# Soft experts of a vision tower: one mixing block per image instead of two, and the down products spread as three per image instead of six per second image

## The reference

```python
slots = jnp.einsum('bnd,bnes->besd', x, dispatch)
h = jax.nn.gelu(jnp.einsum('besd,edh->besh', slots, w1) + b1[None, :, None, :])
y = jnp.einsum('besh,ehd->besd', h, w2) + b2[None, :, None, :]
out = jnp.einsum('besd,bnes->bnd', y, combine)
```

## Time and profile before

| | us |
|---|---|
| median of 3 runs | 1109.38 |
| the runs | 1108.49, 1109.38, 1493.33 |
| the profiled execution | 1109.79 |
| its span (first to last instruction) | 1108.0 |
| soft experts: first hidden matmul to the start of the last down products | 241.06 to 665.51 |
| TensorE busy (share of the span) | 987.2 (89%) |
| ScalarE busy | 661.1 (60%) |
| VectorE busy | 390.4 (35%) |

### The profile page before, as it was taken

The page is one execution under the profiler, slowest core; times in us unless marked ns, Lnnn a source line. Parts: engine busy times, 40 slices in busy tenths (PEclk is TensorE's granted clock), DMA queues, the critical chain, the costliest instruction groups (busy, mean ns, idle before and its releaser), DMA issues. The chain is left out here.

```text
span 1108.0 us, 20060 instructions
## 1 busy us (share of the span) xinstructions
PE 987.2 (89%) x7464; PEld 646.1 (58%) x7464; DVE 390.4 (35%) x1009; ACT 661.1 (60%) x1222; POOL 275.5 (25%) x279
## 2 busy tenths in 40 slices
PE   8869769779999999999999997885159999999997
PEld 8445435433444445444444445354149999999997
DVE  2666958550011111111111113765832222222233
ACT  0566848579888888888888881263114333344332
POOL 0111853230000000000000000100365556565541
PEclk9999879889999999999999999989569999999999
DMA  9000019989655555555555511004469999999985
GB/s 362 7 1 1 1 52 328 321 302 173 125 125 122 124 116 115 124 123 122 118 115 115 117 27 48 0 2 114 165 238 313 334 325 325 322 327 327 326 261 129
DMA packets 76140, 185.37 MB, mean 167 GB/s; under 512 B 15904, under 2 KB 34560, under 8 KB 75784
## 3 DMA queue, kind: packets, MB, share of 16 engines
q1 hardware_dynamic: 63804, 169.44, 51.8%
q0 software_dynamic: 11808, 14.39, 6.3%
q10 hardware_dynamic: 432, 0.26, 0.1%
HBM read 148.36 MB, written 35.69 MB: 166 GB/s over the span
## 5 line engine op out<-in xcount | busy, mean ns | idle before, releaser
L1195 ACT ACTIVATE sle_H<-sle_hp 128x1024 f32<-128x1024 f32 x384 | 367.3, 1024 | 53.7 <-PE sle_hp L1132 53.6
L1649 ACT ACTIVATE ext_H<-ext_hp,ext_bias 128x128 f32<-128x128 f32 x378 | 104.1, 398 | 161.3 <-issue 158.7
L1149 PE MATMUL sle_up<-sle_H,sle_cw 128*32 128x512 f32 (+1 forms) x2048 | 191.4, 492 | 0.0
L1210 DVE STREAM_TRANSPOSE sle_UT<-sle_up 128x256 f32<-128x256 f32 x64 | 37.3, 584 | 289.1 <-PE sle_up L1149 289.1
L1591 PE MATMUL ext_yp<-rmoe_w,ext_H 128*128 128x192 f32 x756 | 133.5, 326 | 1.1 <-issue 0.6
L1591 PEld LDWEIGHTS ext_yp<-rmoe_w,ext_H 128*128 128x128 f32 x756 | 121.5, 190 | 1.7 <-issue 1.7
L1747 POOL DMA_INDIRECT sum<-ext_y,ext_yi x61 | 97.1, 1592 | 92.0 <-DVE ext_gate L1671 48.7
L1117 POOL COPY sle_cw<-keep_CT 128x128 f32<-128x128 f32 x64 | 18.9, 296 | 388.0 <-PE sle_up L1149 387.9
L1132 PE MATMUL sle_hp<-keep_G,keep_dT 99*128 99x512 bf16 (+1 forms) x512 | 101.9, 332 | 8.0 <-PEq L913 6.8
L1149 PEld LDWEIGHTS sle_up<-sle_H,sle_cw 128*32 128x32 f32 x2048 | 53.5, 109 | 87.0 <-issue 73.4
L1132 PE MATMUL sle_hp<-sle_G,sle_dT 99*128 99x512 bf16 (+1 forms) x512 | 99.9, 327 | 1.3 <-ACT sle_H L1195 1.1
(11 more groups left out here) (272 smaller groups left out, 1177.9 us busy)
## 6 DMA issues: line engine op xcount, KB each, us to landing
rmoe_w<-W SPq DMA_DIRECT2D x126, 576.0 KB
pieces<-hid_gp SPq DMA_DIRECT2D x16, 1152.0 KB, 4.9
keep_G<-pieces SPq DMA_DIRECT2D x32, 288.0 KB, 4.1
sle_G<-pieces SPq DMA_DIRECT2D x32, 288.0 KB, 4.1
pieces<-hid_gp SPq DMA_DIRECT2D x8, 768.0 KB, 5.6
keep_G<-pieces SPq DMA_DIRECT2D x32, 192.0 KB, 4.2
sle_G<-pieces SPq DMA_DIRECT2D x32, 192.0 KB, 4.1
keep_CT<-xT SPq DMA_DIRECT2D x6, 512.0 KB, 6.0
```

What stands on the lines that cost most here:

```text
L1149: mm = pe.matmul(to[32 * e:32 * e + 32], cw[:, p, 2 * e + grp, :], H[:, p, h:h + width], start=(p == 0 and grp == 0), stop=(p == 1 and grp ...
L1195: act.activation(H[:, p, WIDTH * k:WIDTH * (k + 1)], hp[k % DEEP][:].rearrange("p a c -> p (a c)"), ACT.Gelu_apprx_tanh).then_inc(gelu_don ...
L1210: dve.transpose(UT[:, par, at // 32:(at + width) // 32, 32 * j:32 * j + 32], src.rearrange("p (b c) -> p b c", c=32)).then_inc(ut_done[ban ...
L1649: act.activation(H[:, q, c, :], hp[q][:, c % 2, (c // 2) * P:(c // 2 + 1) * P], ACT.Gelu, bias=bias[:, q, c:c + 1]).then_inc(gelu_done, 1)
```

## The change

```diff
-    PART = HID // 32 // (TILE_IMAGES // 2)
     BLOCKS = HID // 32
+    PART = BLOCKS // TILE_IMAGES
...
-            def mix(n, p, grp, pair, first_pair, drained):
-
-                pe.wait_ge(gelu_done, OPS * n + 3 * grp + 3)
-                if grp == 0:
-                    pe.wait_ge(cw_ready, n + 1)
...
+            def mix(n, groups):
+
+                p, pair = n % 2, n // 2
+                pe.wait_ge(gelu_done, OPS * (n + 1))
+                pe.wait_ge(cw_ready, n + 1)
+                for grp in range(2):
+                    for bank in (range(2) if p == 0 else (1, 0)):
+                        if grp == 0 and p == 0 and pair:
+                            pe.wait_ge(ut_done[bank], pair)
+                        if grp == 0 and p == 0 and bank == 1 and groups:
+                            pe.wait_ge(y_left, groups)
+                        to, at, width = U[bank]
+                        for e in range(SLOT_E):
+                            h = (4 * grp + e) * HID + at
+                            mm = pe.matmul(to[32 * e:32 * e + 32], cw[:, p, 2 * e + grp, :], H[:, p, h:h + width],
+                                           start=(p == 0 and grp == 0), stop=(p == 1 and grp == 1))
+                        mm.then_inc(mix_done, 1)
+
+            def down(par, pairs, blocks, closed, groups):
 
                 for bank in range(2):
                     pe.wait_ge(ut_done[bank], pairs)
+                if groups:
+                    pe.wait_ge(y_left, groups)
                 for b in blocks:
-                    mm = pe.matmul(yps, UT[:, par, b, :], g.w2[:, b, :], start=(b == blocks[0]), stop=(b == blocks[-1]))
+                    mm = pe.matmul(yps, UT[:, par, b, :], g.w2[:, b, :], start=(closed and b == blocks[0]), stop=(closed and b == blocks[-1]))
                 mm.then_inc(y_ready, 1)
 
             def image(n, m, r, first):
...
+                i, tile = n % TILE_IMAGES, n // TILE_IMAGES
+                groups = max(n - TILE_IMAGES, 0)
+                at = OPS - 1 if i == 0 else n % 2
...
                 for k in range(OPS):
-                    hidden(n, m % 4, k, start)
-                    if p == 0 and k in (0, 3) and not start:
-                        mix(n - 1, 1, k // 3, None, False, None)
-                    if p == 1 and k == 0 and drains:
-                        down((m // TILE_IMAGES - 1) % 2, pair, range(PART * j, PART * (j + 1)))
-                    if p == 1 and k in (2, 4):
-                        mix(n - 1, 0, k // 4, pair, first and m == 1, drained)
+                    hidden(n, n % 4, k, n == 0)
+                    if tile and k == at:
+                        down((tile - 1) % 2, tile * TILE_IMAGES // 2, range(PART * i, PART * (i + 1)), i == 0 or n % 2 == 1, groups)
+                    if k == DEEP and n:
+                        mix(n - 1, groups + 1 if tile else 0)
 
             program(pe, image)
 
-            for grp in range(2):
-                mix(IMAGES - 1, 1, grp, None, False, None)
-            down((TILES - 1) % 2, IMAGES // 2, range(BLOCKS))
+            mix(IMAGES - 1, IMAGES - TILE_IMAGES)
+            down((TILES - 1) % 2, IMAGES // 2, range(BLOCKS), True, IMAGES - TILE_IMAGES)
...
             def image(n, m, r, first):
...
+                i, tile = n % TILE_IMAGES, n // TILE_IMAGES
+                j = i // 2
+                if n % 2 == 0 and n:
+                    leave((tile if j else tile - 1) % 2, (j - 1) % (TILE_IMAGES // 2), n // 2 - 1)
+                if tile:
+                    gather(tile - 1, i, n - TILE_IMAGES + 1)
+                    if i == TILE_IMAGES - 1:
                         finish(Chain(dve, step, base=3 * (tile - 1)), tile - 1)
```

More of the change, by code:

```diff
@@ L1153, in down @@
-            def down(par, pairs, blocks):
+            def mix(n, groups):
[14 more added lines that the diff above has]
+                        mm.then_inc(mix_done, 1)
@@ L1169, in image @@
+                at = OPS - 1 if i == 0 else n % 2
+                if n == 2:
                     pe.wait_ge(more_rows, 32)
                     pe.wait_ge(more_ones, 2)
-                pe.wait_ge(g.image_in[m % 4], 16 * IMAGE_LOADS * (BODY // 4 * r + m // 4 + 1))
+                pe.wait_ge(g.image_in[n % 4], 16 * IMAGE_LOADS * (n // 4 + 1))
                 for k in range(OPS):
-                    hidden(n, m % 4, k, start)
-                    if p == 0 and k in (0, 3) and not start:
-                        mix(n - 1, 1, k // 3, None, False, None)
-                    if p == 1 and k == 0 and drains:
-                        down((m // TILE_IMAGES - 1) % 2, pair, range(PART * j, PART * (j + 1)))
-                    if p == 1 and k in (2, 4):
-                        mix(n - 1, 0, k // 4, pair, first and m == 1, drained)
+                    hidden(n, n % 4, k, n == 0)
[3 more added lines that the diff above has]
+                        mix(n - 1, groups + 1 if tile else 0)
@@ L1245, in _ @@
             leave((TILES - 1) % 2, TILE_IMAGES // 2 - 1, IMAGES // 2 - 1)
-            drained = (TILES - 1) * TILE_IMAGES // 2 + 1
+            drained = IMAGES - TILE_IMAGES + 1
             gather(TILES - 1, 0, drained)
```

## The result

| | before | after |
|---|---|---|
| median of the runs, us | 1112.23 (4 runs) | 1130.37 (4 runs) |
| ratio | 1 | 1.0189, 95% interval 1.0138 to 1.0240 |
| span of the profiled execution, us | 1108.0 | 1128.7 |
| first hidden matmul to the last down products, us | 241.06 to 665.51: 424.5 | 241.09 to 685.66: 444.6 |

The four runs of the kernel before are 1108.49, 1109.38, 1115.08 and 1493.33 us; the last was slow, and the ratio leaves it out: 1130.37 / 1109.38.

The account below looks back on a forecast made before the run. TensorE bounded the kernel from image 8; merged, the buffer ring would: 34 x 6.81 + 21 x 6.83 + 7 x 7.42 = 426.8 us, with start and end +19.6 on 1109.79, less 0.4: 1129.0 us, range 1120 to 1134.

Parts of the forecast that it names:

- The pieces: Lengths read from the timeline before: merged mixing block 2.72 us, three down blocks 0.98, hidden step 0.43 to 0.54.
- H3: Hidden step k = 3, just ahead of the merged mixing block; forecast to be held by a gelu and take 0.54 us.
- The ring: Three PSUM buffers, filled by TensorE, emptied by ScalarE's gelus; forecast to run dry during the merged block and set image time.
- H4: Hidden step k = 4, first behind the merged mixing block; the chain of waits to the next such block starts there.
- Cases A and B: Ordinary images: 34 at 6.81 us, held by the gelu chain; 21 odd ones, down part behind hidden step k = 1, at 6.83.
- Case C: Second image of each tile from the second on, two down parts between merged blocks: 7.42 us, 7 times.
- What was costed at nothing: VectorE's gather per image, 28 more of 0.42 us, plus transposes, image loads and new bank waits: forecast to add no time.
- Rival 1: TensorE's own work decides the soft-expert stretch and the gain arrives: 1094 us; chance 0.05.
- rival 2: TensorE's idling makes its clock fall to 0.97, 0.11 us more per image, 7 us: 1136 us; chance 0.05.
- rival 4: Much smaller loss, slack shared better, e.g. gelus at 0.85: 0.2 us less per image, 1117 us; chance 0.06.
- rival 3: VectorE's new drains hold the merged mixing block: gather 0.5 us later adds 4 us, 1133 us; chance 0.06.
- MM: The merged block of two mixing groups behind hidden step k = 3 of every image, forecast at 2.72 us.

Follow-up runs that it names:

- kernel with the down products spread alone: Changed kernel with the mixing groups back in their old places, three down blocks per image, behind k = 0 in odd images; ratio 1.0125, stretch 429.5 us.
- thinned kernels: A third of the down products left in tiles 2 to 8: changed kernel ratio 1.016, stretch 439.4 us; kernel before ratio 0.977, stretch 394.9 us.
- evenly spaced groups: Kernel before with its four single mixing groups per pair behind k = 1 and 4 of every image, nothing merged; ratio 1.0002, stretch 425.3 us.
- kernel of three blocks per pair: Kernel before with three mixing blocks per image pair, one of them two merged groups of neighbouring images; ratio 0.9969, stretch 419.7 us.
- last version: Kernel before with single groups behind k = 1 and 4 in images 1 to 7, three mixing blocks per pair from image 8; ratio 0.9935, stretch 414.8 us.

## Why the prediction was right

1129.0 us were forecast and 1130.4 measured; against its own profiled execution +19.6 and +20.7. That the two totals agree within 1.4 us is partly luck: 23 runs of the kernel before went from 1104.5 to 1118.9 us. What bears the prediction out is the stretch, +19.6 forecast and +20.1 measured, and its pieces.

- *The pieces.* A merged block is 2.72 us from its start to the next hidden step (304.44 to 307.16), a down part 0.98, a held H3 0.54. All taken from rows of before, all found again.
- *The ring.* H3 at 3.55 us behind H4, worked out by adding one gelu spacing of 0.92 to the two waits of the first tile, is 310.71 - 307.16 = 3.55.
- *Cases A and B*: 6.81 and 6.83 forecast, 6.81 and 6.83 measured. The start of the first merged block was forecast at 249.23 and stood at 249.26.
- *Case C* was put at 7.42 and is 7.51. The term that was too small is the first down part: behind a wait for VectorE it takes 1.08 us (300.55 to 301.63) and not 0.98. Its weight loads start with its matmuls there, at 300.55, where those of the next part start 0.13 ahead (302.37 against 302.50). Seven times 0.09 is 0.6, which covers what was missing within the stretch (0.5); another 0.6 is behind the stretch and was not followed up.
- *What was costed at nothing.* VectorE's drains: in case C the last one ends at 304.18 and the merged block starts at 304.44. Cover of 0.26, where I had 0.35. It held. In the kernel with the down products spread alone a second down part one step behind the first did wait for such a drain (the 0.16 us above).
- *Rival 1* is answered by the thinned kernels, rival 2 by the clock of 1.00 in the changed kernel, rival 4 by the gelu spacing of 0.92. VectorE's drains (rival 3) never held MM; they held a down part, in another kernel. Rival 1 also put the pairs of the first tile at 10.9 us, less than the 12 x 0.92 = 11.0 that ScalarE needs for twelve gelus; 11.33 is what the evenly spaced groups reached.

The chance of 0.22 for more than 2% slower seems fair: the two measurements gave 1.9% and 1.7%, and the interval of the first reaches 2.4%.

On the Trainium skill's rule (TensorEngine Tiling (Array Packing), Key Properties) that a change of tiling mode drains TensorE: the kernel of three blocks per pair shows a way in and out to be worth 0.24 us (13.29 to 13.05). The trace fits the rule, since three hidden steps ahead of down blocks on 128 columns take 1.31 us and ahead of a group on 32-column tiles 1.41; that all of the 0.24 is this drain isn't shown. By the rule alone the change would have gained. It says nothing of what the merged block does to ScalarE.

## What to carry to other kernels

When one engine fills a few buffers that another empties, and also has long work of its own to do, it matters where that work stands, how long each lump is and how often it comes, and not only its sum. Here a block of 2.72 us behind every six hidden steps cost 20 us, and one behind every twelve, with shorter lumps between, gained 5. Don't count only the filling steps on both sides of a lump: three weren't enough in the one kernel and were in the other. Work out the chain that goes once around the buffers (lump, fill, drain times depth, fill) and compare it with TensorE's own work per turn before moving anything. Then look at each moved block for what else it waits for: two down parts too close together, or down blocks close behind the transposes, lost 0.1 to 0.5 us each time.

## What the runs showed of the hardware that was not expected

The part *ahead* of the soft experts, the same instructions in all these kernels, took 240.6 to 249.9 us. It goes with the granted clock of the first 100 us: 240.6 to 241.5 at a mean of 0.97 or 0.98, 245.0 at 0.95, 248.7 to 249.9 at 0.88 (one kernel, at 0.97, took 243.9). Of the kernel before and of the last version, the first 100 us:

```profile
0.00:100.00 100.00, 80.34 (x648) 56.04 (x649) 49.97 (x139) 44.13 (x86) 11.24 (x23) 0.98 0.27 103
```

```profile
0.00:100.00 100.00, 80.72 (x616) 58.18 (x616) 45.74 (x133) 38.79 (x75) 11.24 (x23) 0.88 0.28 103
```

At a mean clock of 0.98 TensorE got through 648 matmuls, at 0.88 through 616. In 12 runs of the last version the whole time went from 1098 to 1112 us while the mean granted clock went from 0.949 to 0.936. The stretch of soft experts repeated to 0.01 us in the two profiles of the changed kernel. So a difference of less than 1% in the total of such a kernel is better read from the stretch that was changed. Why the clock falls early in some executions was not settled.

And the down products of every second image, whose matmuls neither open nor close an accumulation, cost no more than the others: a down part is 0.98 us with and without (308.47 to 309.45 and 302.50 to 303.48).
